# Selective scan: delta times u copied over the partitions from SBUF instead of from a DRAM scratch, rows in channel order

## The chip, the cores and the metric

One core of a Trainium2 chip runs one program of five stages. The metric is the device time of one execution in microseconds; the median of several executions is compared. The engines are TensorE (matmuls, PE in the profile), VectorE (DVE), ScalarE (ACT), GpSimd (POOL) and SyncE (SP), which here only issues transfers. The transfers run on 16 DMA engines.

## The reference

The program computes a gated block, a windowed mixing block, local attention, a selective scan and a channel norm on 96 channels. The change lies in the scan. For 4 images of 64 x 64 pixels and K = 4 directions over the pixels, each of the 96 channels keeps 16 states:

```
x_dbl = einsum('bkdl,kcd->bkcl', xs, x_proj_weight)
dts, Bs, Cs = split(x_dbl, [R, R + N], axis=2)
delta = softplus(einsum('bkrl,kdr->bkdl', dts, dt_projs_weight) + bias)
h = exp(d_t[..., None] * A) * h + (d_t * u_t)[..., None] * B_t[:, :, None, :]
y = einsum('bkdn,bkn->bkd', h, C_t)
```

`d_t * u_t` is a value for each channel; it is multiplied by B for each of the 16 states, so it is wanted 16 times over.

## The kernel before

All stages but the last two are untouched. In `selective_scan` a step is one direction of one image over N = 512 pixels; there are 4 images x 4 directions x 8 chunks = 128 steps. The 96 channels times 16 states are 1536 rows, in 12 groups of 128 partitions (8 channels x 16 states), taken as 6 pairs. A row of a group is state-major: partition s * 8 + d holds state s of channel d. The weights' tables `pick` (copies delta to the rows by a matmul), `y_pick` (sums the states of a channel by a matmul), `w_rep` (B and C to the rows) and `a_logs` follow that order; `selective_scan_layout` makes them on the host.

In a step, for each pair: TensorE replicates delta into PSUM (`replicate`, L2013), ScalarE takes the exponentials (L2150 to L2166), the product of delta times u with B is made by VectorE for pairs 0, 1, 3, 4 (`times_b`, L2313) and by GpSimd for pairs 2 and 5 (L2247), VectorE runs the scan (L2329), GpSimd multiplies by C (L2258), and TensorE sums (L2022).

Delta times u, called du, comes from VectorE as 96 partitions by 512 (`delta_u`, L2300), one step ahead of its use. SP stores it in a DRAM scratch with two halves (`store_du`, L1921) and then replicates it group by group (`replicate_du`, L1936): each of 12 transfers reads 8 channels' rows 16 times from DRAM and writes 128 partitions of one of 8 ring slots of `du_rep`. A slot is written again when the product that read it is done (the wait at L1930 or L1932). The single buffer `du` is written again when the store of the step before has landed (the wait at L2299).

SP's queue goes in this order for a step: replications 8 to 11 of this step; the store for the next one; its replications 0 and 1; a wait for TensorE; four restacks (`restack`, L1910, 96 KB each, SBUF to SBUF, 48 partitions to 48), which bring delta to where TensorE reads it; replications 2 to 7. Every transfer of the scan is issued by SP and goes through one queue.

Two lines of other stages serve for comparison. The local attention loads its values in eight transfers behind each other, each into 16 partitions (L1298, `v[chalf][at:at + HP_PAIRS]` with HP_PAIRS = 16, rows of 1216 B, 152 KB, from DRAM). The channel norm at the end stores its result from 96 partitions of SBUF (L2399, rows of 4096 B, 384 KB).

Of the kernel before, what the change touches and what calls it, by code (L numbers as in the profile page):

```python
# [15 lines left out]
ALU = mybir.AluOpType  # L16
ACT = mybir.ActivationFunctionType
AX_X = mybir.AxisListType.X
F32 = mybir.dt.float32
# [4 lines left out]
B, C, H, W = 4, 96, 64, 64  # L24
HW = H * W
T = B * HW
N = 512
# [1714 lines left out]
    }  # L1742


def selective_scan(nc, w, X, du_d):
    K, S, R, DL = 4, 16, 6, 8
    G = C // DL
    Q = 48
# [15 lines left out]
    with ExitStack() as ctx:  # L1764
# [20 lines left out]
        one_e = sb("l3_one_e", [C + 1, N])  # L1785
        log_e = sb("l3_log_e", [C, N])
        dd = log_e
        du = sb("l3_du", [C, N])
        parts = sb("l3_parts", [C, 2, N], F32R)
        stacked = sb("l3_stacked", [C, 2, PARTS, N], F32R)  # L1790
        du_rep = sb("l3_du_rep", [128, RING, N])
# [19 lines left out]
        s_d, s_hi, s_lomm, s_lo, s_du = (sem("l3_" + n) for n in (  # L1811
            "delta_summed", "delta_high", "low_mm", "low", "du"))
        s_bcp, s_pbu = sem("l3_b_copied"), sem("l3_pool_bu")
        s_dus = sem("l3_du_stored")
        s_stack = [sem(f"l3_stacked{i}") for i in range(2)]
        s_dur = [sem(f"l3_du_replicated{i}") for i in range(RING)]
        s_c, s_ccp, s_b = sem("l3_c_mm"), sem("l3_c_copied"), sem("l3_b_mm")
        s_rep, s_join, s_da, s_bu, s_h, s_hc, s_ymm, s_ysum, s_y = (sem("l3_" + n) for n in (
            "delta_replicated", "joint_da", "da", "bu", "h", "hc", "y_triple", "y_whole", "y_taken"))

        H0, HC0, YMM0, Y0, HI0, LO0, CCP0, DU0, DUS0 = 2, PAIRS, TRIPLES, 2, 1, 1, 1, 1, 16
        BU0, PBU0 = 2 * NB, 2 * NP
        weights = [(xp_dt, "xp_dt"), (dt_w, "dt_w_T"), (w_rep[:], "w_rep"), (pick_f, "pick"),
                   (y_pick[:], "y_pick"), (plus[0:C], "ident"), (a_neg[:], "a_logs"), (cols[:], "cols")]
# [6 lines left out]
        def u_of(b, k, c):  # L1831
            at = chunk_of(k, c) * N
            return X[:, bass.ds(b * HW + at, N)] if k % 2 == 0 else xt[:, bass.ds(at, N)]
# [65 lines left out]
        @block.sync  # L1899
        def _(sp_):  # L1900
            for dst, src in weights:
                sp_.dma_start(dst, w[src]).then_inc(s_w, 16)

            def restack(m, par):

                sp_.wait_ge(s_lo, m + 1 + LO0)
                sp_.nop(nofuse=True)
                for part in range(2):
                    for q in range(PARTS):
                        sp_.dma_start(stacked[part * Q:(part + 1) * Q, par, q].bitcast(F32),  # L1910
                                      parts[q * Q:(q + 1) * Q, part].bitcast(F32)).then_inc(s_stack[par], 16)

            def store_du(m, par):

                sp_.wait_ge(s_du, m + 1 + DU0)
                sp_.nop(nofuse=True)
                sp_.wait_ge(s_bu, NB * (m - 1) + BU0)
                sp_.nop(nofuse=True)
                sp_.wait_ge(s_pbu, NP * (m - 1) + PBU0)
                sp_.nop(nofuse=True)  # L1920
                sp_.dma_start(du_d[par], du[:]).then_inc(s_dus, 16)  # L1921

            def replicate_du(n, par, i):

                if i == 0:
                    sp_.wait_ge(s_dus, 16 * (n + 1) + DUS0)
                    sp_.nop(nofuse=True)
                user, step_of = (i - RING) % G // 2, (i - RING) // G
                if user in POOL_PAIRS:
                    sp_.wait_ge(s_pbu, NP * (n + step_of) + POOL_PAIRS.index(user) + 1 + PBU0)  # L1930
                else:
                    sp_.wait_ge(s_bu, NB * (n + step_of) + DVE_PAIRS.index(user) + 1 + BU0)  # L1932
                sp_.nop(nofuse=True)
                src = du_d[par, GRP[i] * DL:(GRP[i] + 1) * DL]
                src = bass.AP(src.tensor, src.offset, [[0, S], [N, DL], [1, N]])
                sp_.dma_start(du_rep[:, ring_at(par, i)], src).then_inc(s_dur[ring_at(par, i)], 16)  # L1936

            def step(n, par, more):
                for i in range(RING, G):
                    replicate_du(n, par, i)  # L1940
                if more:
                    store_du(n + 1, 1 - par)
                    for i in range(2):
                        replicate_du(n + 1, 1 - par, i)
                    sp_.wait_ge(s_rep, G * n)
                    sp_.nop(nofuse=True)
                    restack(n + 1, 1 - par)
                    for i in range(2, RING):
                        replicate_du(n + 1, 1 - par, i)

            store_du(0, 0)
            for i in range(2):
                replicate_du(0, 0, i)
            restack(0, 0)
            for i in range(2, RING):
                replicate_du(0, 0, i)
            step(0, 0, True)
            with sp_.Fori(0, B * STEPS // 2 - 1) as i:
                step(2 * i + 1, 1, True)
                step(2 * i + 2, 0, True)  # L1960
            step(B * STEPS - 1, 1, False)
# [314 lines left out]
        def _(dve):  # L2276
# [14 lines left out]
            dve.tensor_scalar(plus[C:C + 1], plus[C:C + 1], -1.0, None, ALU.mult)  # L2291
            dve.wait_ge(s_setup_cp, 7)
            dve.tensor_scalar(d_diag[:], ident, d_sum[:], None, ALU.mult).then_inc(s_setup_cp, 1)
            for s, credit in ((s_bu, BU0), (s_h, H0), (s_dus, DUS0), (s_du, DU0)):
                dve.sem_inc(s, credit)

            def delta_u(m, b, k, c):
                dve.wait_ge(s_hi, m + 1 + HI0)
                dve.wait_ge(s_dus, 16 * m + DUS0)  # L2299
                dve.tensor_tensor(du[:], p_bc[0:C, :], u_of(b, k, c), ALU.mult).then_inc(s_du, 1)  # L2300

            def loaded(n, i, par):
                dve.wait_ge(s_dur[ring_at(par, i)], ring_count(n, par, i))
# [28 lines left out]
            def step(b, n, k, c, par, n1, n2, before):  # L2332
                times_b(n, 1, par)
                scan(n, k, c, 0, par)
                scan(n, k, c, 1, par)
                if n1:
                    if k == 0 and isinstance(c, int) and c == CHUNKS - 1:
                        dve.wait_ge(s_xt, CHUNKS * b + CHUNKS)
                    delta_u(n + 1, *n1)
                times_b(n, 3, par)  # L2340
                scan(n, k, c, 2, par)
                times_b(n, 4, par)
                scan(n, k, c, 3, par)
                scan(n, k, c, 4, par)
                if n1:
                    times_b(n + 1, 0, 1 - par)
                scan(n, k, c, 5, par)

            delta_u(0, 0, 0, 0)
            times_b(0, 0, 0)  # L2350
            all_steps(step)(dve)
            dve.wait_ge(s_y, B * STEPS + Y0)
# [114 lines left out]
def selective_scan_layout(w):  # L2467

    g = {n[len("L3_conv_"):]: a for n, a in w.items() if n.startswith("L3_conv_")}
    K, S, R, DL, Q = 4, 16, 6, 8, 48  # L2470
    G = C // DL
    xp = g["x_proj_weight"]
    bc = xp[:, R:].reshape(K, 2, S, 1, C)
    pick = np.zeros((C // Q, Q, Q // DL, S, DL), np.float32)
    for j in range(Q // DL):
        for dl in range(DL):
            pick[:, j * DL + dl, j, :, dl] = 1
    y_pick = np.zeros((S, DL, 4, 4 * DL), np.float32)
    for grp in range(4):
        for dl in range(DL):  # L2480
            y_pick[:, dl, grp, grp * DL + dl] = 1
    return {
        "xp_dt": xp[:, :R].transpose(1, 0, 2),
        "dt_w_T": g["dt_projs_weight"].transpose(2, 0, 1),
        "w_rep": np.broadcast_to(bc, (K, 2, S, DL, C)).reshape(K, 2, S * DL, C).transpose(3, 0, 1, 2),
        "pick": pick.reshape(C, Q // DL, S * DL),
        "y_pick": y_pick.reshape(S * DL, 4, 4 * DL),
        "ident": np.eye(C, dtype=np.float32),
        "a_logs": g["A_logs"].reshape(K, G, DL, S).transpose(3, 2, 0, 1).reshape(S * DL, K * G),
        "cols": np.concatenate([g["dt_projs_bias"].T, g["Ds"].reshape(K, C).T], 1),  # L2490
        "center": np.eye(C, dtype=np.float32) - np.float32(1 / C),
        "mean_w": np.full((C, C), 1 / C, np.float32),
        "cols_out": np.stack([g["ln_g"].reshape(C), g["ln_b"].reshape(C)], 1),
    }
# [20 lines left out]
def build(nc, x, w, out):  # L2515

    qkv_d = nc.dram_tensor("qkv_scratch", (4 * C, B, HP * WP), F32, kind="Internal").ap()
    v_d = nc.dram_tensor("v_scratch", (C, XH, B, HP * VX), F32, kind="Internal").ap()
    o_d = nc.dram_tensor("o_scratch", (C, XH, B, H * XW), F32, kind="Internal").ap()
    x_d = nc.dram_tensor("x_scratch", (C, T), F32, kind="Internal").ap()  # L2520
    du_d = nc.dram_tensor("du_scratch", (2, C, N), F32, kind="Internal").ap()
    with ExitStack() as ctx:
        front = ctx.enter_context(nc.sbuf_tensor("front", [128, T], F32))
        X = front[0:C]
        gated_ssm_block(nc, x, w["L0"], X)
        s_xd = ctx.enter_context(nc.semaphore("x_stored"))
        with ExitStack() as early:
            qkv = AttentionFront(nc, early, w["L2"], X, qkv_d, v_d, x_d, s_xd)
            sedenion_block(nc, w["L1"], X, qkv)
            attention_qkv(nc, X, qkv, qkv_d, v_d)  # L2530
        attention_heads(nc, w["L2"], qkv_d, v_d, o_d, front, x_d, s_xd)
    clear_semaphores(nc)
    with ExitStack() as ctx:
        X = ctx.enter_context(nc.sbuf_tensor("x_back", [C, T], F32))
        attention_out(nc, w["L2"], X, o_d, x_d)
        selective_scan(nc, w["L3"], X, du_d)
        channel_norm_out(nc, w["L3"], X, out)


# [19 lines left out]
```

## Time and profile before

| | us |
|---|---|
| median of 3 timed runs | 5180.48 |
| lowest and highest of them | 5178.35, 5186.24 |
| the profiled execution | 5180.92 |
| its span, first to last instruction | 5179.0 |
| the scan in it, first to last step (about) | 2671 to 5085 |

The profiled execution lies 0.44 us above the median. A row that begins with a line number is one group of instructions; its busy time, the mean length of one and the idle time just before them follow. Rows of stretches give the busy time of each engine within so many microseconds, then the granted TensorE clock as a share, the mean busy share of the 16 DMA engines and GB/s. A transfer's landing time is counted from its issue, so it holds the time behind others in the queue.

### The profile page before, as it was taken

The numbers are of one execution on the slowest core, as the hardware profiler recorded it, in microseconds if no ns is written. First come the engines' busy times: TensorE is split into PE (matmuls) and PEld (weight loads), VectorE is DVE, ScalarE is ACT, GpSimd is POOL, SyncE is SP. The second block draws the span as 40 slices with busy tenths as digits, with TensorE's granted clock in tenths as the row PEclk, the third lists the DMA queues.
The fourth block names the chain that finished last, engine by engine and source line by source line (L and its number), as shares of the span: only waits on it lengthen the run. The fifth ranks groups of instructions, "written<-read, shape, count | busy, mean of one in ns | idle before, by whom it ended". The sixth has DMA issues, their size and how long they took to land. (4 is left out here: it accounts for less than half of the span.)

```text
span 5179.0 us, 68498 instructions
## 1 busy us (share of the span) xinstructions
PE 4463.9 (86%) x15210; PEld 2075.2 (40%) x15210; DVE 4213.2 (81%) x3398; ACT 3166.5 (61%) x6678; POOL 4131.1 (80%) x1990
## 2 busy tenths in 40 slices
PE   6998897975999999992888888889898888889887
PEld 2332553632666666661542223223232233222332
DVE  3666555553389999999559999999999999999995
ACT  6886555542111111110568888888888888888886
POOL 3665555543388989889659999999999999999993
PEclk9998998987999999996889999999999999999998
DMA  2000102228677877782437888787888878888883
GB/s 54 1 1 14 53 27 69 67 87 227 148 149 140 150 137 150 143 150 27 104 75 198 200 201 203 192 198 202 198 203 194 202 197 200 201 201 201 198 203 94
DMA packets 389223, 733.04 MB, mean 142 GB/s; under 512 B 78460, under 2 KB 119464, under 8 KB 375912
## 3 DMA queue, kind: packets, MB, share of 16 engines
q1 hardware_dynamic: 388968, 730.17, 60.0%
q8 instruction: 95, 1.56, 0.1%
q14 instruction: 160, 1.31, 0.1%
HBM read 594.18 MB, written 82.32 MB: 131 GB/s over the span
## 5 line engine op out<-in xcount | busy, mean ns | idle before, releaser
L2258 POOL TENSOR_TENSOR l_hc<-l_h,l_c_rep 128x1024 f32<-128x1024 f32 x768 | 1797.5, 2369 | 22.6 <-DVE l_h L2329 11.2
L1436 POOL TENSOR_TENSOR front<-l2b_v,front 128x1568 f32<-128x1568 f32 x276 | 936.7, 3457 | 235.6 <-ACT front L1397 119.1
L2329 DVE TENSOR_TENSOR_SCAN l_h<-l_p,l_h,l_bu 128x1024 f32<-128x1024 f32 x448 | 1026.2, 2327 | 5.1 <-ACT l_bu L2166 3.7
L2013 PE MATMUL l_p<-l_stacked,l_pick 96*128 96x512 f32 x1536 | 561.4, 447 | 224.6 <-DVE l_h L2329 203.9
L1484 DVE TENSOR_REDUCE l2b_osum<-front 128x32 f32<-128x1568 f32 x384 | 665.6, 1780 | 62.6 <-POOL front L1436 58.8
L2247 POOL TENSOR_TENSOR l_pool_bu<-l_du_rep,l_b_sb 128x1024 f32<-128x1024 f32 x256 | 607.3, 2372 | 40.3 <-DMA l_du_rep<-du_scratch 40.1
L2313 DVE TENSOR_TENSOR l_bu<-l_du_rep,l_p 128x1024 f32<-128x1024 f32 x512 | 610.7, 1193 | 27.7 <-DMA l_du_rep<-du_scratch 21.4
L1389 ACT ACTIVATE l2b_logits<-l2b_conv,l2b_this_b 98x512 f32<-98x512 f32 x96 | 66.2, 689 | 863.3 <-PE l2b_conv L1354 863.3
L2013 PEld LDWEIGHTS l_p<-l_stacked,l_pick 96*128 96x128 f32 x1536 | 243.6, 190 | 805.0 <-DVE l_h L2329 643.8
L2022 PE MATMUL l_p<-l_hc,l_y_pick 128*32 128x512 f32 x3072 | 521.7, 606 | 4.9 <-POOL l_hc L2258 4.9
L2329 DVE TENSOR_TENSOR_SCAN l_h<-l_p,l_h,l_pool_bu 128x1024 f32<-128x1024 f32 x224 | 523.2, 2336 | 3.3 <-ACT l_pool_bu L2166 2.8
L2153 ACT ACTIVATE l_p<-l_p,l_a_neg 128x512 f32<-128x512 f32 x768 | 513.9, 669 | 0.0
L2151 ACT ACTIVATE l_p<-l_p,l_a_neg 128x511 f32<-128x511 f32 x768 | 508.4, 662 | 0.0
L1354 PE MATMUL l2b_conv<-l2b_img_high,l2b_w_conv_high 128*98 128x512 f32 x1344 | 357.6, 420 | 33.6 <-DMA l2b_img_low<-qkv_scratch 33.6
L2150 ACT ACTIVATE l_joint_da<-l_p,l_a_neg 128x1 f32<-128x1 f32 x768 | 204.5, 266 | 237.5 <-PE l_p L2013 235.2
L1354 PE MATMUL l2b_conv<-l2b_img_high,l2b_w_conv_low 128*98 128x512 f32 x1344 | 338.8, 403 | 0.0
L1354 PE MATMUL l2b_conv<-l2b_img_low,l2b_w_conv_high 128*98 128x512 f32 x1344 | 337.4, 402 | 0.0
L1354 PEld LDWEIGHTS l2b_conv<-l2b_img_high,l2b_w_conv_high 128*98 128x98 f32 x1344 | 231.5, 173 | 142.2 <-issue 34.4
L1354 PEld LDWEIGHTS l2b_conv<-l2b_img_high,l2b_w_conv_low 128*98 128x98 f32 x1344 | 219.6, 163 | 103.7
L1354 PEld LDWEIGHTS l2b_conv<-l2b_img_low,l2b_w_conv_high 128*98 128x98 f32 x1344 | 219.8, 164 | 102.1
L956 POOL TENSOR_TENSOR l1b_h_h_low<-l1b_h_h,l1b_h_h_high 128x512 fp32r<-128x512 f32 x96 | 124.8, 1312 | 151.3 <-DVE l1b_h_h_high L910 151.3
L2022 PEld LDWEIGHTS l_p<-l_hc,l_y_pick 128*32 128x32 f32 x3072 | 87.6, 108 | 385.7 <-issue 310.5
(271 smaller groups left out, 8880.5 us busy)
## 6 DMA issues: line engine op xcount, KB each, us to landing
l_du_rep<-du_scratch SPq DMA_DIRECT2D x1536, 256.0 KB, 4.9
l2b_img_high<-qkv_scratch SPq DMA_DIRECT2D x192, 306.2 KB, 5.7
l2b_img_low<-qkv_scratch SPq DMA_DIRECT2D x192, 306.2 KB, 9.5
l_stacked<-l_parts SPq DMA_DIRECT2D x512, 96.0 KB, 3.3
l2b_v<-v_scratch SPq DMA_DIRECT2D x192, 152.0 KB, 6.5
qkv_scratch<-l2a_strip SPq DMA_DIRECT2D x32, 840.0 KB, 5.2
du_scratch<-l_du SPq DMA_DIRECT2D x128, 192.0 KB, 2.1
l_w_raw<-L_w_sed SPq DMA_DIRECT2D x32, 576.0 KB, 3.8
```

The lines of the kernel that those rows point to most:

```text
L1354: mm = pe.matmul(p_conv[n % 2][:], w_conv[w_part][:, g, dx, :], img[x_part][:, b % 2, row:row + 2 * CP - 1:2, dx:dx + W], start=(at == 0), ...
L1436: return eng.tensor_tensor(dst.rearrange("q x (dy dx) -> q x dy dx", dx=WIN), window, attn_half[:, :, unit % 2].rearrange("q x (dy dx) -> ...
L1484: dve.tensor_reduce(osum[:, half, unit // 2, unit % 2, :], prod[which][:], AX_X, ALU.add).then_inc(s_sum, 1)
L2013: pe.matmul(p_da[p % 2][:, e, :], pick[:, GRP[i] % (Q // DL), :], stacked[:, par, GRP[i] * DL // Q, :], start=True, stop=True).then_inc(s_ ...
L2022: mm = pe.matmul(p_y[q * 32:(q + 1) * 32, :], y_pick[:, t, :], hc[:, hc_at(par, i // 2) + i % 2, :], start=(t == 0), stop=False)
L2150: act.activation(joint_da[:, p % 2:p % 2 + 1], da[:, e, at:at + 1], ACT.Exp, scale=rate(2 * p + e)).then_inc(s_join, 1)
L2151: act.activation(da[:, e, rest], da[:, e, rest], ACT.Exp, scale=rate(2 * p + e))
L2153: act.activation(da[:, 1 - e, :], da[:, 1 - e, :], ACT.Exp, scale=rate(2 * p + 1 - e))
L2247: pool.tensor_tensor(pool_bu[:], du_rep[:, slot:slot + 2, :], b_sb[:, par, :].unsqueeze(1).to_broadcast([128, 2, N]), ALU.mult).then_inc(s ...
L2258: pool.tensor_tensor(hc[:, slot:slot + 2, :], h[:, 2 * p:2 * p + 2, :], c_rep[:, par, :].unsqueeze(1).to_broadcast([128, 2, N]), ALU.mult) ...
L2313: dve.tensor_tensor(bu[:, at % 2], du_rep[:, slot:slot + 2, :], p_b[par].unsqueeze(1).to_broadcast([128, 2, N]), ALU.mult).then_inc(s_bu, 1)
L2329: dve.tensor_tensor_scan(flat(h[:, 2 * p:2 * p + 2, :]), flat(p_da[p % 2]), flat(of), state, ALU.mult, ALU.add).then_inc(s_h, 1)
```

## The change

The store to the DRAM scratch and its semaphore are gone. `du` gets two halves by the parity of the step, and VectorE writes one or the other; before it does so it waits for GpSimd's products of two steps before. A replication now takes as its source the 8 partitions of `du` that hold its channels, each row read 16 times before the next partition's. Written to the 128 partitions in that order, the rows become channel-major: partition d * 16 + s. The tables are permuted to match and keep their shapes. SP waits for du itself (s_du) ahead of replication 0, where it waited for the store.

```diff
-        du = sb("l3_du", [C, N])
+        du = sb("l3_du", [C, 2, N])
...
-            def store_du(m, par):
-
-                sp_.wait_ge(s_du, m + 1 + DU0)
-                sp_.nop(nofuse=True)
-                sp_.wait_ge(s_bu, NB * (m - 1) + BU0)
-                sp_.nop(nofuse=True)
-                sp_.wait_ge(s_pbu, NP * (m - 1) + PBU0)
-                sp_.nop(nofuse=True)
-                sp_.dma_start(du_d[par], du[:]).then_inc(s_dus, 16)
-
             def replicate_du(n, par, i):
 
                 if i == 0:
-                    sp_.wait_ge(s_dus, 16 * (n + 1) + DUS0)
+                    sp_.wait_ge(s_du, n + 1 + DU0)
                     sp_.nop(nofuse=True)
...
-                src = du_d[par, GRP[i] * DL:(GRP[i] + 1) * DL]
-                src = bass.AP(src.tensor, src.offset, [[0, S], [N, DL], [1, N]])
+                src = du[GRP[i] * DL:(GRP[i] + 1) * DL, par, :]
+                src = bass.AP(src.tensor, src.offset, [list(src.ap)[0], [0, S], [1, N]])
                 sp_.dma_start(du_rep[:, ring_at(par, i)], src).then_inc(s_dur[ring_at(par, i)], 16)
 
             def step(n, par, more):
                 for i in range(RING, G):
                     replicate_du(n, par, i)
                 if more:
-                    store_du(n + 1, 1 - par)
                     for i in range(2):
                         replicate_du(n + 1, 1 - par, i)
...
-            def delta_u(m, b, k, c):
+            def delta_u(m, b, k, c, par):
                 dve.wait_ge(s_hi, m + 1 + HI0)
-                dve.wait_ge(s_dus, 16 * m + DUS0)
-                dve.tensor_tensor(du[:], p_bc[0:C, :], u_of(b, k, c), ALU.mult).then_inc(s_du, 1)
+                dve.wait_ge(s_pbu, NP * (m - 1) + PBU0)
+                dve.tensor_tensor(du[:, par, :], p_bc[0:C, :], u_of(b, k, c), ALU.mult).then_inc(s_du, 1)
...
-    pick = np.zeros((C // Q, Q, Q // DL, S, DL), np.float32)
+    pick = np.zeros((C // Q, Q, Q // DL, DL, S), np.float32)
     for j in range(Q // DL):
         for dl in range(DL):
-            pick[:, j * DL + dl, j, :, dl] = 1
+            pick[:, j * DL + dl, j, dl, :] = 1
...
-        "a_logs": g["A_logs"].reshape(K, G, DL, S).transpose(3, 2, 0, 1).reshape(S * DL, K * G),
+        "a_logs": g["A_logs"].reshape(K, G, DL, S).transpose(2, 3, 0, 1).reshape(S * DL, K * G),
```

`y_pick` and `w_rep` swap the same two axes.

## Rows read from the trace of the kernel before

**Rows 1.** head of the page: span, engines' busy time, share, instructions

```profile
span 5179.0 us, 68498 instructions
PE 4463.9 (86%) x15210; PEld 2075.2 (40%) x15210; DVE 4213.2 (81%) x3398; ACT 3166.5 (61%) x6678; POOL 4131.1 (80%) x1990
```

**Rows 2.** busy time by stretch (the scan), columns in its first line

```profile
core 0: us, PE busy (x) PEld busy (x) DVE busy (x) ACT busy (x) POOL busy (x), PEclk, DMA share, GB/s
2740.00:5040.00 2300.00, 2034.33 (x6737) 687.44 (x6738) 2274.56 (x1348) 1995.47 (x4958) 2278.65 (x980) 1.00 0.81 200
```

**Rows 3.** groups by line in 2740 to 5040 us, columns in its first line

```profile
line engine op names shapes xcount | busy us, mean ns | idle before us <-releasers
L2329 DVE TENSOR_TENSOR_SCAN l_h<-l_p,l_h,l_bu 128x1024 f32<-128x1024 f32 x430 | 984.7, 2327 | 4.0 <-ACT l_bu L2166 3.0 <-DVE l_bu L2313 0.3
L2313 DVE TENSOR_TENSOR l_bu<-l_du_rep,l_p 128x1024 f32<-128x1024 f32 x490 | 584.4, 1193 | 17.8 <-DMA l_du_rep<-du_scratch 11.5 <-issue 6.1
L2258 POOL TENSOR_TENSOR l_hc<-l_h,l_c_rep 128x1024 f32<-128x1024 f32 x735 | 1720.3, 2370 | 19.0 <-issue 10.9 <-DVE l_h L2329 7.6
```

**Rows 4.** one line's instructions, L1921, the du store

```profile
L1921 SPq DMA_DIRECT2D du_scratch<-l_du x128: 309/317/328, 2671.9 to 5058.4; - x128
DMA to landing us min/median/max: 2.0/2.1/4.3
```

**Rows 5.** L1936, the replications, the same view; then waits of engines on them

```profile
L1936 SPq DMA_DIRECT2D l_du_rep<-du_scratch x1536: 513/545/1988, 2674.1 to 5072.3; - x192
DMA to landing us min/median/max: 3.0/4.9/7.7
...
POOL l_pool_bu L2247 <- DMA l_du_rep<-du_scratch: 40.1, 8, 37.9
...
  DVE l_bu L2313: 21.4, 27
```

**Rows 6.** what SP waited for in 2740 to 5040 us: total, times, longest

```profile
SPq L1916 <- DVE l_du L2300: 464.0, 123, 5.2
SPq L1927 <- DMA du_scratch<-l_du: 228.2, 122, 3.9
```

**Rows 7.** DMA packets, queue (packets, MB, share), issues, 4000 to 4100 us

```profile
DMA packets 11211, 20.02 MB, mean 200 GB/s; under 512 B 1477, under 2 KB 1477, under 8 KB 11202
...
q1 hardware_dynamic: 11202, 19.92, 82.0%
...
l_du_rep<-du_scratch SPq DMA_DIRECT2D x67, 256.0 KB, 5.2
l_stacked<-l_parts SPq DMA_DIRECT2D x21, 96.0 KB, 3.4
du_scratch<-l_du SPq DMA_DIRECT2D x5, 192.0 KB, 2.1
```

**Rows 8.** busy time by stretch within scan steps, columns as in rows 2

```profile
4016.80:4017.40 0.60, 0.60 (x2) 0.00 (x1) 0.60 (x2) 0.60 (x2) 0.60 (x1) 1.00 0.80 307
4022.50:4024.00 1.50, 1.20 (x4) 0.79 (x5) 1.50 (x2) 0.75 (x3) 1.50 (x2) 1.00 1.08 254
4018.90:4020.20 1.30, 0.95 (x3) 0.68 (x4) 1.30 (x2) 1.30 (x4) 1.30 (x1) 1.00 0.95 189
```

**Rows 9.** the same view: attention's value loads, then the output stores

```profile
1296.00:1300.00 4.00, 4.00 (x19) 2.70 (x18) 0.00 (x0) 0.00 (x1) 0.00 (x0) 1.00 1.06 172
5105.00:5175.00 70.00, 58.66 (x123) 17.44 (x121) 39.05 (x64) 60.20 (x94) 0.00 (x0) 0.99 0.29 84
```

**Rows 10.** L1298, the value loads; queue and issues in 5105 to 5175 us

```profile
L1298 SPq DMA_DIRECT2D l2b_v<-v_scratch x192: 312/321/3448, 1279.2 to 2385.1; - x192
...
DMA to landing us min/median/max: 3.2/6.5/21.5
...
q1 hardware_dynamic: 1659, 5.87, 28.6%
out<-l3n_result SPq DMA_DIRECT2D x15, 384.0 KB, 3.0
```

More of the change, by code:

```diff
@@ L1742, in local_attention_layout, with selective_scan @@
     }
-def selective_scan(nc, w, X, du_d):
+def selective_scan(nc, w, X):
     K, S, R, DL = 4, 16, 6, 8
@@ L1813, in selective_scan @@
         s_bcp, s_pbu = sem("l3_b_copied"), sem("l3_pool_bu")
-        s_dus = sem("l3_du_stored")
         s_stack = [sem(f"l3_stacked{i}") for i in range(2)]
@@ L1819, in selective_scan @@
             "delta_replicated", "joint_da", "da", "bu", "h", "hc", "y_triple", "y_whole", "y_taken"))
-        H0, HC0, YMM0, Y0, HI0, LO0, CCP0, DU0, DUS0 = 2, PAIRS, TRIPLES, 2, 1, 1, 1, 1, 16
+        H0, HC0, YMM0, Y0, HI0, LO0, CCP0, DU0 = 2, PAIRS, TRIPLES, 2, 1, 1, 1, 1
         BU0, PBU0 = 2 * NB, 2 * NP
@@ L1949, in step @@
                         replicate_du(n + 1, 1 - par, i)
-            store_du(0, 0)
             for i in range(2):
@@ L2293, in _ @@
             dve.tensor_scalar(d_diag[:], ident, d_sum[:], None, ALU.mult).then_inc(s_setup_cp, 1)
-            for s, credit in ((s_bu, BU0), (s_h, H0), (s_dus, DUS0), (s_du, DU0)):
+            for s, credit in ((s_bu, BU0), (s_h, H0), (s_du, DU0)):
                 dve.sem_inc(s, credit)
-            def delta_u(m, b, k, c):
+            def delta_u(m, b, k, c, par):
                 dve.wait_ge(s_hi, m + 1 + HI0)
-                dve.wait_ge(s_dus, 16 * m + DUS0)
-                dve.tensor_tensor(du[:], p_bc[0:C, :], u_of(b, k, c), ALU.mult).then_inc(s_du, 1)
+                dve.wait_ge(s_pbu, NP * (m - 1) + PBU0)
+                dve.tensor_tensor(du[:, par, :], p_bc[0:C, :], u_of(b, k, c), ALU.mult).then_inc(s_du, 1)
             def loaded(n, i, par):
@@ L2338, in step @@
                         dve.wait_ge(s_xt, CHUNKS * b + CHUNKS)
-                    delta_u(n + 1, *n1)
+                    delta_u(n + 1, *n1, 1 - par)
                 times_b(n, 3, par)
@@ L2347, in step @@
                 scan(n, k, c, 5, par)
-            delta_u(0, 0, 0, 0)
+            delta_u(0, 0, 0, 0, 0)
             times_b(0, 0, 0)
@@ L2473, in selective_scan_layout @@
     bc = xp[:, R:].reshape(K, 2, S, 1, C)
-    pick = np.zeros((C // Q, Q, Q // DL, S, DL), np.float32)
+    pick = np.zeros((C // Q, Q, Q // DL, DL, S), np.float32)
     for j in range(Q // DL):
         for dl in range(DL):
-            pick[:, j * DL + dl, j, :, dl] = 1
-    y_pick = np.zeros((S, DL, 4, 4 * DL), np.float32)
+            pick[:, j * DL + dl, j, dl, :] = 1
+    y_pick = np.zeros((DL, S, 4, 4 * DL), np.float32)
     for grp in range(4):
         for dl in range(DL):
-            y_pick[:, dl, grp, grp * DL + dl] = 1
+            y_pick[dl, :, grp, grp * DL + dl] = 1
     return {
@@ L2484, in selective_scan_layout @@
         "dt_w_T": g["dt_projs_weight"].transpose(2, 0, 1),
-        "w_rep": np.broadcast_to(bc, (K, 2, S, DL, C)).reshape(K, 2, S * DL, C).transpose(3, 0, 1, 2),
+        "w_rep": np.broadcast_to(bc, (K, 2, S, DL, C)).swapaxes(2, 3).reshape(K, 2, S * DL, C).transpose(3, 0, 1, 2),
         "pick": pick.reshape(C, Q // DL, S * DL),
@@ L2520, in build @@
     x_d = nc.dram_tensor("x_scratch", (C, T), F32, kind="Internal").ap()
-    du_d = nc.dram_tensor("du_scratch", (2, C, N), F32, kind="Internal").ap()
     with ExitStack() as ctx:
@@ L2535, in build @@
         attention_out(nc, w["L2"], X, o_d, x_d)
-        selective_scan(nc, w["L3"], X, du_d)
+        selective_scan(nc, w["L3"], X)
         channel_norm_out(nc, w["L3"], X, out)
```

## The prediction

> **What bounds the kernel now.** I read the page's shares first: VectorE and GpSimd are each busy for about four fifths of the 5179.0 us span [rows 1]. A share over the whole program mixes five blocks, so the next view is the busy time in the scan alone. In 2300 us of it VectorE works 2274.56 us and GpSimd 2278.65 us, 99% each, while the 16 DMA engines are busy 0.81 of the time at 200 GB/s [rows 2]. The groups by line tell what the two do: VectorE's scans and products with B, GpSimd's products with C, and hardly any idle time before any of them [rows 3]. So the scan is bound by two compute engines, and the transfers lie beside them with a fifth of their time to spare. The pace of a step comes from the du store, one per step: 128 starts from 2671.9 to 5058.4 us [rows 4], (5058.4 - 2671.9) / 127 = 18.79 us a step. The profiled execution took 5180.92 us, 0.44 us over the median of the three timed runs, so I add to 5180.92.
>
> What the present transfers cost those engines is in the view of the replicated tile: waits for it come to 40.1 us on GpSimd in 8 places, 37.9 us of it in one, and 21.4 us on VectorE in 27 [rows 5]. The latter is all that a better path could give back in the steps, 0.4% of the kernel.
>
> **What is removed.** Per step one store (0.317 us of SP's issue, 2.1 us to land [rows 4]), and SP's wait for it, 228.2 us in 122 steps, 1.87 us each [rows 6]. That wait hides: SP issues 12 replications (0.545 us each [rows 5]) and four restacks in a step of 18.79 us and spends 464.0 us in all waiting for du itself [rows 6]. With the store gone SP waits for du and then issues; what is next late is du, as now. I cost the removal at nothing between steps, and 2 to 4 us once at the first step, where nothing covers the trip.
>
> **What is added at no cost.** du has two halves, VectorE's multiply writes one or the other: same instruction, same size. In front of it stands a wait for GpSimd's products of two steps before instead of the wait for the store. Behind it in VectorE's order stand the product for pair 3 and all later scans, but GpSimd is at most about a step behind, so it is met long before. If it were not, each late step would cost up to one GpSimd product, 2.37 us [rows 3]. The tables for channel-major rows (pick, y_pick, w_rep, a_logs) keep their shapes; matmuls and activations see the same columns. No row gives a reason for a price there, either way.
>
> **What is changed in kind: the 12 replications.** Each still writes 128 partitions with 256 KB. The source was 8 rows in DRAM, walked with the 16 copies outermost; now it is 8 partitions of SBUF, walked partition by partition, each read 16 times. The trace of before has no transfer like it, so I bound its rate.
>
> - Fast end: the source doesn't matter. The best stretch of the scan moves 307 GB/s at a DMA share of 0.80, which is 307 / (16 x 0.80) = 24.0 GB/s for an engine at work; with all engines loaded on DRAM sources it is 254 GB/s [rows 8]. At 254 GB/s a replication takes 262144 B / 254 = 1.03 us, and the new kernel differs by nothing.
> - Slow end: four neighbouring partitions give together no more than one engine takes, 24.0 GB/s. Then 8 partitions give 48 GB/s, and a replication takes 5.46 us.
>
> Two stretches show that few partitions on the SBUF side do slow a transfer. The value loads of the attention stage go into 16 partitions each, eight transfers queued behind each other [rows 10]; there the engines are fully busy (share 1.06) and move 172 GB/s, where the scan moves 254 GB/s [rows 8, 9]. The output stores read 96 partitions of SBUF: 84 GB/s at a share of 0.29, 18.1 GB/s for a busy engine, three quarters of 24.0 [rows 9, 10]. The restacks (48 partitions on both sides) go at 189 GB/s with a share of 0.95 [rows 8], 12.4 for a busy engine.
>
> The nearest row is the 16-partition one, as it too has several neighbours served at once and a deep queue: 172 / 16 = 10.75 GB/s a partition, 86 GB/s for 8. I take that; one replication is 262144 / 86 = 3.05 us. It lies between the ends 1.03 and 5.46 us.
>
> The Trainium skill has two rules that speak against this change. "DMA: Bandwidth & Descriptors", section "Why a DMA increments its semaphore by 16 and not by 1", says that a transfer runs on the largest number of engines up to 16 that divides the outermost count of both patterns: 16 copies and 128 partitions made 16 before, 8 partitions and 128 make 8 now. The trace agrees for before: 1477 packets under 512 B for 93 transfers, 16 closing writes each [rows 7]. "SBUF — State Buffer", section "Door 1: The DMA port swizzle", puts four neighbouring partitions on one port of about 27 GB/s, so 8 partitions reach two; by that figure alone a replication would take 4.8 us and the kernel about 10.4 ms, an estimate from the page. The stores above agree in kind.
>
> **The sum.** A step's transfers are 12 replications, 12 x 3.05 = 36.6 us, and four restacks, 4 x 98304 B / 189 GB/s = 2.08 us [rows 8]: 38.7 us. They are one queue, and a step can't be shorter than they are; VectorE's and GpSimd's 18.6 us hide below. So 38.7 - 18.79 = 19.9 us a step, 128 steps, 2543 us. 5180.92 + 2543 = 7724 us. The eight-slot ring keeps the queue full, since a slot is freed as soon as its pair is multiplied; a bubble per step would add, not take away.
>
> Own range: if eight engines keep what each has now in a loaded queue, 254 / 16 x 8 = 127 GB/s, the step is 24.8 + 2.1 = 26.9 us, total 6210 us. Halfway in rate between 86 and 48 (the geometric mean, 64 GB/s), 4.10 us, step 51.2 us, total 9335 us.
>
> **Rivals.**
> 1. *Lockstep.* Each four neighbours really share one engine's rate, and the readers stay together from transfer to transfer: 48 GB/s, step 65.5 + 2.1 = 67.6 us, 5180.92 + 128 x 48.8 = 11430 us. For it: the stores' 18.1 against 24.0 GB/s, and that nothing but queue depth pulls readers apart. Against: 172 GB/s into 16 partitions is 43 GB/s for four neighbours, so there they did spread. Between it and my own range lies the same mechanism with less spread.
> 2. *Fewer engines, but nothing shared.* One reader to each partition at 24.0 GB/s: 192 GB/s, 1.365 us, step 16.4 + 2.1 = 18.5 us, 98% of 18.79. It just fits; waits for a late transfer then add from nothing to about 1 us a step, 5180 to 5310 us. Against it stand the stores, which lose a quarter with far more partitions.
> 3. *No effect in the steps.* Reads from SBUF go at 254 GB/s or more: transfers stay at or under 0.81 of the time, VectorE and GpSimd stay the bound, 5170 to 5191 us.
> 4. *Faster, the other side.* SBUF reads at the 307 GB/s of the best stretch: a step's transfers are 12 x 0.85 + 2.1 = 12.3 us, so the waits of 61.5 us for the replicated tile vanish (21.4 us of VectorE's at most in the steps, and the trip at the start), down to about 5150 us. It decides once a replication costs less than the present 1.03 us. For it: the store and its landing are gone, and DRAM is left out of the path. Against: 8 source partitions would have to serve at the full rate that 96 did not in the stores.
>
> **Chances.** Forecast and its own range (6210 to 9335 us) 0.50; lockstep and the stretch up to it (9335 to 11450) 0.22; a smaller loss between 5310 and 6210 us 0.08; rival 2 above the bound of no change 0.08; rival 3 0.08; faster 0.04. A measurement of this kernel tells about 0.2% (10 us) from no change; so faster 0.04, same 0.08, slower 0.88. The range that leaves out 2 in 10 is 5310 to 11430 us (0.50 + 0.22 + 0.08): it cuts the cases near the present time.
>
> **What will show it.** After the change, time to landing of the replication: now 4.9 us in the middle [rows 5]; with eight queued at 3.05 us each it should be near 24 us, at lockstep over 40, and under 6 if rival 3 or 4 holds. VectorE's busy share in the scan falls from 99% to about half, with its idle time before the product with B put down to the DMA of the replicated tile. GB/s in the scan falls to (12 x 262144 + 4 x 98304) / 38.7 us = 91 GB/s. The packets under 512 B tell the engines: 8 per replication instead of 16 if there are fewer, while the packets' mean time tells sharing: about 0.085 us for 2 KB at 24.0 GB/s without any, 0.19 us in my forecast on eight engines, 0.34 us in lockstep. TensorE has 2034.33 us of work in 2300 [rows 2] and is hidden at 38.7 us a step even at half its clock. I am wrong if VectorE stays at 99%: then the rate per partition doesn't carry over from writes of 16 partitions to reads of 8, which is the weakest step here.

## The result: 8725 us, 1.68 times the time before

The changed kernel takes 8725.32 us (median of 4 runs, 8715.54 to 8742.45) where the kernel before takes 5182.59 us beside it: a ratio of 1.684, 95% interval 1.682 to 1.686. The forecast was 7724 us. It went the way forecast, and 1.39 times as far: 3543 us instead of 2543.

The head of the page of the changed kernel answers [rows 1]; VectorE's and GpSimd's busy times are nearly those of before, 4256.7 and 4129.1 us, in a span that is 3543 us longer.

```profile
span 8722.4 us, 67607 instructions
PE 5626.5 (65%) x15210; PEld 2496.6 (29%) x15210; DVE 4256.7 (49%) x3398; ACT 3228.8 (37%) x6678; POOL 4129.1 (47%) x1990
```

Busy time in the changed kernel's scan, with the columns of [rows 2]: VectorE works 41% of it instead of 99%, the DMA engines are busy 0.47 of the time, the granted TensorE clock is 0.61.

```profile
2740.00:8500.00 5760.00, 3194.74 (x6813) 1109.11 (x6808) 2349.02 (x1364) 2083.06 (x5020) 2303.25 (x992) 0.61 0.47 76
```

The groups by line of the same stretch, as [rows 3], and the replications' own row, as [rows 5]. L2300 is VectorE's product with B and L2234 GpSimd's; L1925 issues the replications.

```profile
L2300 DVE TENSOR_TENSOR l_bu<-l_du_rep,l_p 128x1024 f32<-128x1024 f32 x496 | 605.8, 1221 | 3414.9 <-DMA l_du_rep<-l_du 3414.9
L2234 POOL TENSOR_TENSOR l_pool_bu<-l_du_rep,l_b_sb 128x1024 f32<-128x1024 f32 x248 | 582.2, 2348 | 2385.8 <-DMA l_du_rep<-l_du 2385.8
...
L1925 SPq DMA_DIRECT2D l_du_rep<-l_du x1536: 657/3109/4813, 2672.4 to 8614.7; - x192
```

All of VectorE's idle time in the stretch is ahead of the product with B, and all of it is put down to the replication. The work before and behind it is as long as it was. The replications start from 2672.4 to 8614.7 us; from the first of step 0 to the last of step 127 are 127 11/12 steps, so a step takes 5942.3 / 127.92 = 46.5 us. The same sum on [rows 5] gives 18.75 us for before. Below, steps are worked out in this way from each kernel's row.

The transfers in 1000 us of it, as [rows 7] (there 100 us):

```profile
DMA packets 40711, 76.67 MB, mean 77 GB/s; under 512 B 3425, under 2 KB 3425, under 8 KB 40677
...
q1 hardware_dynamic: 40677, 76.31, 46.9%
...
l_du_rep<-l_du SPq DMA_DIRECT2D x259, 256.0 KB
l_stacked<-l_parts SPq DMA_DIRECT2D x86, 96.0 KB, 6.3
```

Two things are read here. The closing writes (under 512 B) are 3425: 259 replications with 8 each and 86 restacks with 16 make 3448, with 16 each they would make 5520. So a replication runs on eight engines, and the share of 0.47 of sixteen is eight engines busy nearly all the time (a small part of it is the restacks', on 16). And a packet of 2 KB, a few of them the restacks', takes 0.469 x 16 x 1000 us / (40677 - 3425) = 0.201 us, where at 24.0 GB/s [rows 8] it would take 0.085.

### The profile page after: what moved, and what is told of

Same layout as the page of the kernel before. It is cut to its first block and busy times, and to the rows that moved or that the text cites. A ratio compares the mean times of both kernels' runs of the same rounds, so it can differ in the third digit from the quotient of the medians.

```text
span 8722.4 us, 67607 instructions
## 1 busy us (share of the span) xinstructions
PE 5626.5 (65%) x15210; PEld 2496.6 (29%) x15210; DVE 4256.7 (49%) x3398; ACT 3228.8 (37%) x6678; POOL 4129.1 (47%) x1990
## 5 line engine op out<-in xcount | busy, mean ns | idle before, releaser
L2000 PE MATMUL l_p<-l_stacked,l_pick 96*128 96x512 f32 x1536 | 947.0, 715 | 2658.0 <-DVE l_h L2316 1894.7
L2300 DVE TENSOR_TENSOR l_bu<-l_du_rep,l_p 128x1024 f32<-128x1024 f32 x512 | 625.4, 1221 | 3533.2 <-DMA l_du_rep<-l_du 3533.2
L2234 POOL TENSOR_TENSOR l_pool_bu<-l_du_rep,l_b_sb 128x1024 f32<-128x1024 f32 x256 | 601.0, 2348 | 2506.4 <-DMA l_du_rep<-l_du 2506.4
L2000 PEld LDWEIGHTS l_p<-l_stacked,l_pick 96*128 96x128 f32 x1536 | 412.5, 308 | 3601.4 <-DVE l_h L2316 2413.3
L2009 PE MATMUL l_p<-l_hc,l_y_pick 128*32 128x512 f32 x3072 | 720.3, 811 | 5.4 <-POOL l_hc L2245 5.4
L2153 ACT ACTIVATE l_bu<-l_joint_da,l_bu,l_h 128x1 f32<-128x1 f32 x448 | 173.5, 387 | 1176.3 <-DVE l_bu L2300 1176.3
L2153 ACT ACTIVATE l_pool_bu<-l_joint_da,l_pool_bu,l_h 128x1 f32<-128x1 f32 x224 | 86.6, 387 | 662.7 <-POOL l_pool_bu L2234 662.7
L1993 PE MATMUL l_p<-l_log_e,l_plus 96*96 96x512 f32 x256 | 258.8, 1115 | 3.6 <-DVE l_du L2287 3.6
```

The source lines that it names most:

```text
L2000: pe.matmul(p_da[p % 2][:, e, :], pick[:, GRP[i] % (Q // DL), :], stacked[:, par, GRP[i] * DL // Q, :], start=True, stop=True).then_inc(s_ ...
L2009: mm = pe.matmul(p_y[q * 32:(q + 1) * 32, :], y_pick[:, t, :], hc[:, hc_at(par, i // 2) + i % 2, :], start=(t == 0), stop=False)
L2153: act.activation(of, joint_da[:, p % 2:p % 2 + 1], ACT.Identity, bias=of, scale=before).then_inc(s_da, 1)
L2234: pool.tensor_tensor(pool_bu[:], du_rep[:, slot:slot + 2, :], b_sb[:, par, :].unsqueeze(1).to_broadcast([128, 2, N]), ALU.mult).then_inc(s ...
L2300: dve.tensor_tensor(bu[:, at % 2], du_rep[:, slot:slot + 2, :], p_b[par].unsqueeze(1).to_broadcast([128, 2, N]), ALU.mult).then_inc(s_bu, 1)
```

## The experiments

The theory to test: the loss is neighbours among the source partitions being served together, four at a time, at one engine's rate, softened only as the readers of one transfer move on to other partitions. The rivals: eight engines instead of 16, or reads from SBUF as such. Each experiment was timed once; the kernel before, timed beside it, took 5180.51 to 5185.34 us.

**The walk alone, source in DRAM.** The kernel before with channel-major rows: the eight rows are outermost, the store is kept.

```diff
-                src = bass.AP(src.tensor, src.offset, [[0, S], [N, DL], [1, N]])
+                src = bass.AP(src.tensor, src.offset, [[N, DL], [0, S], [1, N]])
```

with the tables as in the change.

> The kernel before, with the store to DRAM kept, but rows channel by channel: the DRAM source is walked with the 8 rows outermost, as the changed kernel walks its 8 partitions. This takes the source in SBUF away and leaves the walk. Theory (shared source partitions cost the time; eight engines work instead of 16): 8 closing writes for a replication instead of 16, 2 KB packets of about 0.085 to 0.13 us, 12 x 16 packets x 0.09 us plus restacks and store = 17.3 + 1.8 + 0.6 = 19.7 us a step, in all 5250 to 5600 us. Rival (the walk with 8 outermost alone, that is the number of engines, costs it): about 8700 us, as the changed kernel.

Measured: 5558.02 us. Its packets in 4000 to 5000 us and its replications' row:

```profile
DMA packets 91845, 172.13 MB, mean 172 GB/s; under 512 B 8083, under 2 KB 8083, under 8 KB 91781
...
q1 hardware_dynamic: 91781, 171.45, 50.6%
...
L1936 SPq DMA_DIRECT2D l_du_rep<-du_scratch x1536: 574/579/1144, 2675.6 to 5449.9; - x192
```

A step is 2774.3 / 127.92 = 21.7 us, a packet 0.506 x 16000 / (91781 - 8083) = 0.097 us. The share of 0.506, a part of it the store's and the restacks' on 16 engines, is eight engines with little pause. So the walk on eight engines, with the store and SP's waits for it still there, costs some 375 us; it is not the 3543.

**SBUF, partitions four apart.** The changed kernel, eight partitions that lie 4 apart.

```diff
-                src = du[GRP[i] * DL:(GRP[i] + 1) * DL, par, :]
+                at = GRP[i] // 4 * 32 + GRP[i] % 4
+                src = du[at:at + 29:4, par, :]
```

> The changed kernel, its replications reading 8 partitions that lie 4 apart (t, t+4, ... t+28 of a block of 32) instead of 8 neighbours. The tables are not permuted to match, so channels are mixed up between rows; amount and shape of the work are the same. Theory (neighbours share, in fours): no two of the eight share any more, packets of 0.085 us, 12 x 16 x 0.085 + restacks 2 = 18.3 us a step, in all 5180 to 5450 us. Rival (reading SBUF for a replication is slow whichever partitions are read): about 8700 us.

Measured: 5336.17 us.

```profile
DMA packets 93762, 176.36 MB, mean 176 GB/s; under 512 B 7912, under 2 KB 7912, under 8 KB 93704
...
q1 hardware_dynamic: 93704, 175.73, 55.8%
...
L1926 SPq DMA_DIRECT2D l_du_rep<-l_du x1536: 604/616/1347, 2679.8 to 5227.0; - x192
```

Same engine count, same bytes, same source memory: a packet takes 0.558 x 16000 / (93704 - 7912) = 0.104 us, half of 0.201, and a step 19.9 us. Which partitions are read makes 3389 us of the 3543. Between kernels that both use eight engines the change's idea pays: this is 222 us under the run from DRAM.

**One source for all.** Every replication reads partitions 0 to 7.

```diff
-                src = du[GRP[i] * DL:(GRP[i] + 1) * DL, par, :]
+                src = du[0:DL, par, :]
```

> The changed kernel, every replication reading the same 8 partitions 0 to 7; the other channels' values are left out. Theory (eight neighbours are served at two engines' rate, and only readers that have moved on to another transfer's partitions get more): no reader can get away from the others, 5.3 to 5.5 us a replication, 12 x 5.4 + 2 = 67 us a step, in all 11.0 to 11.6 ms, with packets near 0.33 us. Rival (the rate hangs on the single partition or on the engine): no change from the changed kernel, 8725 us.

Measured: 11188.89 us.

```profile
q1 hardware_dynamic: 28801, 53.93, 47.8%
...
L1925 SPq DMA_DIRECT2D l_du_rep<-l_du x1536: 658/4528/4759, 2676.9 to 11069.7; - x192
```

A step is 8392.8 / 127.92 = 65.6 us. Less 2.1 us of restacks that is 5.3 us a replication, 49.5 GB/s for eight neighbours. This is lockstep: the readers can't get away from each other, and four neighbours get 24.8 GB/s, near the 24.0 of one engine at work [rows 8]. "SBUF — State Buffer" in the Trainium skill, section "Door 1: The DMA port swizzle", puts about 27 GB/s on one port of four neighbours; the run agrees within a tenth. In the changed kernel the share of engines at work is the same, 0.47 to 0.48, and the readers do get away, as it is faster.

**Another order of the groups.** The second block is taken two groups on, so that neighbours in the queue never read p and p + 32. `y_pick` follows.

```diff
-    GRP = [(i % YT) * YJ + i // YT for i in range(G)]
+    GRP = [(i % YT) * YJ + (i // YT + 2 * (i % YT == 1)) % YJ for i in range(G)]
```

> The changed kernel with another order of the groups: the second block of channels is taken two groups on, so that transfers behind each other never read partitions p and p+32. All tables follow. Theory (the readers of a transfer pull apart from transfer to transfer, and neighbours in the queue that read p and p+32 keep them together, as these share too): a replication falls from 3.7 us to about 3.0, in all 7600 to 8300 us. If partitions p and p+32 do not share: no change, 8725 us. Strict lockstep in all transfers would give no change either.

Measured: 8024.99 us.

```profile
q1 hardware_dynamic: 46035, 86.34, 46.6%
...
L1925 SPq DMA_DIRECT2D l_du_rep<-l_du x1536: 657/2813/4362, 2676.3 to 7917.4; - x192
```

A step is 41.0 us, 5.5 less, and 700 us go with a mere change of order. So what a transfer costs hangs on its neighbours in the queue. That it is p and p + 32 which share is the theory's reading; its forecast was met, but no order that moves another block was run.

**A ring of four slots.**

```diff
-    RING = 8
+    RING = 4
```

> The changed kernel with a ring of 4 slots in place of 8, so that fewer replications can stand in the queue. In the changed kernel a replication lands 11 to 15 us after its issue and its issue takes 3.1 us instead of 0.545, so about four stand in the queue at a time. Theory (how far readers pull apart hangs on how many transfers are queued): less of a queue, nearer to lockstep; between 3.9 and 5.4 us a replication, 9.3 to 10.9 ms. Rival (the queue's depth doesn't matter for the rate): about 8.7 to 9.0 ms, the difference being waits for slots alone.

Measured: 9075.25 us, under the range of the theory and a little over the rival's. Half the slots cost 4%. The two rows, SP's issue and what SP waited for in 3000 to 5000 us:

```profile
L1925 SPq DMA_DIRECT2D l_du_rep<-l_du x1536: 604/1493/4602, 2678.4 to 8965.5; - x192
...
SPq L1922 <- DVE l_bu L2300: 359.8, 124, 4.1
SPq L1922 <- POOL l_pool_bu L2234: 188.2, 41, 5.0
```

SP now waits for slots where in the changed kernel it waits for nothing at all and is held in the issue itself (3.109 us in the middle, against 0.545 before [rows 5]). The ring of eight was never filled. Counted at the end of each issue, in steps 6 to 121, at most four replications of the changed kernel had not landed, mostly three (903 of 1392); with four slots it is mostly three as well (1159 of 1392). The expectation missed because it counted on the slots for the depth, which they did not change much; so whether the depth sets how far readers part stays open.

**The restacks out of SP's queue.** ScalarE issues them behind its copy of the low part. SP's wait for TensorE ahead of them goes too; in the changed kernel SP waited for nothing there. All else is as changed.

```diff
-                    sp_.wait_ge(s_rep, G * n)
-                    sp_.nop(nofuse=True)
-                    restack(n + 1, 1 - par)
...
                     low(n + 1)
+                    restack(n + 1, 1 - par)
```

> The changed kernel, its four restacks of a step issued by ScalarE behind its copy of the low part instead of by SP between replications 1 and 2. In the changed kernel the replication behind the restacks lands on all its readers within 0.2 us and takes 5 us or more, later ones spread by 3 to 7 us and take 2 to 5. Theory (the restacks empty the queue and bring the readers together again, so that spreading starts afresh in each step): without that a step falls from 46.5 to 40 to 43 us, 7.9 to 8.3 ms. Rival (the restacks cost only their own bytes): 2 us or less a step, 8.45 to 8.73 ms.

Measured: 7241.46 us, better than both expectations.

```profile
q1 hardware_dynamic: 47341, 91.26, 46.4%
q10 hardware_dynamic: 7424, 11.41, 4.2%
...
L1916 SPq DMA_DIRECT2D l_du_rep<-l_du x1536: 657/2460/4740, 2679.3 to 7133.0; - x192
```

A step is 34.8 us, 11.6 less than 46.5, for transfers whose own bytes are 2.1 us. Why, the landings show. No view of the profile gives them for transfers on eight engines; the times below are those of the semaphore events in the two traces, one line for a replication of step 51 in the order of the queue: issue, first and last of the eight engines' landings, their distance, and the time since the transfer before landed (us).

```
changed kernel                               restacks with ScalarE
 i  issue    first    last     apart since    issue    first    last     apart since
 1  5038.12  5045.58  5050.62   5.04  3.01    4462.59  4470.85  4474.96   4.12  2.65
    (four restacks)
 2  5050.21  5057.02  5057.23   0.21  6.61    4464.56  4472.41  4477.25   4.84  2.29
 3  5050.99  5060.03  5062.54   2.51  5.31    4467.40  4474.11  4480.93   6.81  3.67
 4  5051.84  5065.48  5067.03   1.55  4.49    4471.83  4478.10  4483.31   5.21  2.38
 5  5055.93  5066.91  5071.09   4.18  4.06    4473.82  4479.40  4485.45   6.05  2.14
 6  5060.30  5068.09  5075.89   7.80  4.80    4476.45  4483.05  4489.33   6.28  3.88
 7  5064.84  5075.30  5078.53   3.23  2.64    4480.25  4487.61  4491.56   3.94  2.23
 8  5069.28  5076.85  5080.55   3.70  2.02    4482.89  4489.10  4493.51   4.40  1.95
```

In the changed kernel replication 2 is issued at 5050.21, when replication 1 is all but landed (5050.62): during the 12 us from replication 1 to 2 SP was held in the restacks' issue and the queue ran empty. All eight engines then start together, land within 0.21 us of each other, and the transfer takes lockstep's time. The next ones spread out and get faster, down to 2.0 us; then the next step's restacks bring them together again. With the restacks elsewhere no transfer shown lands within less than 3.9 us, and none takes lockstep's time.

Steps 6 to 121 of both traces agree. In the changed kernel replication 2 is always issued less than 1.4 us before replication 1 has landed, so the queue has all but run empty; its engines land 0.27 us apart in the median, and replications 2 to 6 land 6.62, 5.26, 4.51, 3.60 and 4.71 us behind the one before. With the restacks elsewhere replication 2 lands 4.46 us apart, and the five take 1.93, 3.93, 2.32, 1.88 and 3.90.

Is it the empty queue itself that costs the time, or that it gathers the readers? The run with one source tells them apart. It has the same restacks in the same place, and its queue runs empty there too, but its readers are together anyway. Its replications land 5.30 us behind each other in the median; 12 of them are 63.6 us of the 65.6, so restacks and empty queue cost 2.0 us a step, about the price of their bytes. Most of the 11.6 us in the changed kernel is thus the readers' start from one point, an estimate from the two runs.

**Partitions two apart, tables to match.**

```diff
-                src = du[GRP[i] * DL:(GRP[i] + 1) * DL, par, :]
+                at = GRP[i] // 2 * 16 + GRP[i] % 2
+                src = du[at:at + 15:2, par, :]
...
```

> The changed kernel with the channels of a group two apart (8 of 16 neighbours), tables to match: two readers share instead of four. Theory: lockstep would be 0.168 us a packet, 12 x 16 x 0.168 + 2 = 34.3 us a step; with the share of it that the changed kernel takes (46.5 of 67) some 24 us. So 5850 to 7200 us, likeliest near 6000. Rival (only the number of distinct partitions counts, eight in both): 8725 us.

Measured: 6493.31 us, within the range and over the likeliest.

```profile
q1 hardware_dynamic: 64891, 121.68, 49.5%
...
L1926 SPq DMA_DIRECT2D l_du_rep<-l_du x1536: 657/1826/2510, 2669.7 to 6388.4; - x192
```

A step is 29.1 us: two that share instead of four, and the time lies between those for none (19.9) and four (46.5). The number of distinct partitions is eight in all three.

**All three edits together.**

> The three edits together: channels of a group two apart, the other order of the groups, restacks issued by ScalarE. Theory: readers in pairs that soon part, 12 x 16 x 0.09 to 0.11 us + 2 = 19.5 to 23 us a step, 5300 to 5750 us; the floor is the kernel with sources 4 apart, 5336 us. If the three don't add up: as the best of them alone.

Measured: 6190.07 us, over the range of the theory and under the best of the three alone; the expectation was wrong. Waits in 4000 to 5000 us, and the restacks' issue:

```profile
ACT l_joint_da L2133 <- issue: 259.3, 37, 8.2
DVE l_h L2314 <- ACT l_bu L2149: 251.4, 75, 8.3
...
L2115 ACTq DMA_DIRECT2D l_stacked<-l_parts x512: 511/2189/2687, 2675.7 to 6068.7; - x171
```

A restack's issue takes 2.189 us on ScalarE while the engines are full, four of them in a row, and behind them in ScalarE's order stands its work for pair 3, from the first exponential (L2133) to the column that the scan needs (L2149). VectorE's scan waits for that, 251.4 us in 1000. No wait of VectorE for the replication is left near the top; one wait took the place of the other.

**Two of the three, restacks with SP.** Partitions two apart and the other order.

> Channels of a group two apart and the other order of the groups, with the restacks left with SP. In the run that had all three edits (6190 us) ScalarE stood some 6 us a step in issuing the restacks, and VectorE waited for it. If that wait ate what the other two edits gave, this kernel is near or below it: the order took 20% off the loss of the changed kernel, 20% off the 1310 us lost at two apart gives 6230 us, 6000 to 6300. If the order does nothing where only pairs share: 6450 to 6500 us.

Measured: 5891.96 us, a step of 3115.4 / 127.92 = 24.4 us, below the run with all three by 298 us and under the range expected.

```profile
L1926 SPq DMA_DIRECT2D l_du_rep<-l_du x1536: 609/1665/2564, 2672.6 to 5788.0; - x192
```

So ScalarE's wait had eaten more than the restacks' move gave. Of the kernels run, none is under the kernel before.

## Why the prediction was right in its direction and short in size

- *The bound and the sum.* Right: the two compute engines' 18.6 us went below the transfers, and a step is as long as its queue; eight engines were busy 94% of the time.
- *The removal at nothing.* Right as far as it can be seen: SP has no wait left in the scan. What it would have saved between steps is hidden by the queue; with sources four apart, where it isn't, SBUF is 222 us ahead of DRAM with the same walk.
- *The rate, 86 GB/s from 16-partition writes.* The number came out near, by luck; the reason for it did not hold. With the restacks elsewhere SP's queue moves 91.26 MB in 1000 us, which is 262144 / 91260 = 2.87 us a replication against 3.05. But there is no one rate for a partition: eight are read in every run, and a step is 46.5, 29.1 or 19.9 us as they lie side by side, two or four apart. Nor did the row chosen, the value loads, show that few partitions slow a transfer, as its packets are smaller. The kernel before, 1296 to 1300 us:

```profile
DMA packets 616, 0.69 MB, mean 172 GB/s; under 512 B 72, under 2 KB 613, under 8 KB 613
...
q1 hardware_dynamic: 616, 0.69, 106.1%
```

A packet, nearly all of them rows of 1216 B, took 1.061 x 16 x 4 / (616 - 72) = 0.125 us; in the scan one of 2 KB took 0.82 x 16 x 100 / (11202 - 1477) = 0.135 us [rows 7]. So the lower GB/s can come from the size of the packets alone.

- *The step that failed: four restacks at 2.08 us, added to the rest.* They were priced by their bytes. In SP's queue they cost 11.6 us a step, 9.5 more, as they emptied it and gathered the readers; the replications, 34.8 us without them against 36.6, took back 1.8. The sentence on the ring said that it keeps the queue full and that a bubble would add; the bubble was there in each step read. 46.5 us instead of 38.7 a step, 7.8 x 128 = 998 us, is the 1000 us that the forecast missed.
- *Landing time near 24 us.* Wrong: the medians by place in the step are 7.0 to 15.2 us. It was worked out from eight queued transfers; the queue held at most four, and the rest of the wait stood in SP's issue.
- *The other signs.* A packet at 0.19 us was forecast, 0.201 is measured; 91 GB/s, 76 measured; VectorE at half, 41% measured; eight closing writes, measured. The rule on the number of engines in the Trainium skill, "DMA: Bandwidth & Descriptors", section "Why a DMA increments its semaphore by 16 and not by 1", held: 3425 closing writes where eight for a replication make 3448.
- *The rivals.* Lockstep was forecast at 11430 us; where nothing lets the readers part it is 11189. Eight engines and nothing shared was forecast at 5180 to 5310; with sources four apart it is 5336. Both were met closely, and the changed kernel lies between them.
- *Faster.* The condition was a replication under 1.03 us. Even unshared, eight engines need 16 packets of 0.104 us each, 1.66 us.

## What to carry to other kernels

What a replication from SBUF costs hangs on which partitions it reads: ask how many of them lie in the same four neighbours, and what the next transfer in the queue reads, before asking how many bytes move. Spacing the eight sources by four took 3389 us off here without one byte less (that run left the tables as they were; with tables to match, two apart was run, not four). That fewer partitions would cost more was not run: all had eight. And a small transfer in a full queue is not priced by its bytes: look at what its issue holds up, and on whose engine.

## What the runs showed of the hardware that I had not expected

- The issue of a transfer is no fixed price: 0.545 us on SP before [rows 5], 3.109 us in the middle in the changed kernel, 4.528 us in lockstep, and 0.616 with sources four apart. When the engines are behind, the issuing engine stands; on ScalarE, 2.189 us for each restack.
- Readers that share part by themselves within a few transfers: from replication 2 on, the engines of one land 0.27, 2.55, 1.77, 4.22 and 7.39 us apart (medians of steps 6 to 121). With the other order of the groups it is 0.22, 1.71, 4.26, 5.25 and 3.26, so what stands next to each other in the queue has a part in how far.
- TensorE's granted clock was 1.00 (2.4 GHz) in the scan before [rows 2] and 0.61 in the mean of the changed one, between its levels of 1.2 and 2.4 GHz, with TensorE at work 55% of the time instead of 88%; its matmul for the replication of delta took 715 ns instead of 443. It was not on the path: VectorE's idle time was all for the transfer.
